# A second self attention whose negated maxima are written into the score banks by ScalarE

## What is computed

```
q = (q_in @ wq).reshape(b, n, H, HD).transpose(0, 2, 1, 3)
...
scores = jnp.einsum('bhnd,bhld->bhnl', q, k) * scale
probs = jax.nn.softmax(scores, axis=-1)
out = jnp.einsum('bhnl,bhld->bhnd', probs, v)
out = out.transpose(0, 2, 1, 3).reshape(b, n, H * HD)
return out @ wo + bo
```

## Time and profile before

| | us |
|---|---|
| median of 3 runs | 4218.95 |
| lowest and highest | 4212.62, 4226.44 |
| span of the profiled execution | 4217.9 |
| TensorE busy | 3909.5 (93%) |
| VectorE busy | 2770.9 (66%) |
| GpSimd busy | 1859.2 (44%) |
| ScalarE busy | 1839.2 (44%) |

### The profile page before, as it was taken

How to read it: one execution, slowest core, us unless ns; L and a number is a source line. 1 busy time by engine, 2 the same in 40 slices (tenths; PEclk the granted TensorE clock), 3 DMA queues, 4 the chain that set the end, 5 groups by cost and what they waited for, 6 DMA issues and landing times. The chain is left out here.

```text
span 4217.9 us, 64445 instructions
## 1 busy us (share of the span) xinstructions
PE 3909.5 (93%) x24639; PEld 2598.3 (62%) x24639; DVE 2770.9 (66%) x4547; ACT 1839.2 (44%) x2746; POOL 1859.2 (44%) x1203
## 2 busy tenths in 40 slices
PE   3799999994998997998999999999999979999899
PEld 2533443433557886884666666666666647777787
DVE  6599999953536654435676767676766737665665
ACT  1267777771443333442333333333333334444333
POOL 1288970001203002005777777877787753222200
PEclk9789999996779998997999999999999989999899
DMA  4734434405622005883211111121112010000100
GB/s 159 180 56 77 59 57 48 42 2 94 102 43 52 22 13 197 306 308 103 75 51 51 64 63 51 51 76 51 51 51 76 26 31 10 10 10 1 42 15 17
DMA packets 314421, 294.96 MB, mean 70 GB/s; under 512 B 133420, under 2 KB 237292, under 8 KB 313860
## 3 DMA queue, kind: packets, MB, share of 16 engines
q1 hardware_dynamic: 311460, 281.88, 25.7%
q0 software_dynamic: 2656, 8.97, 0.7%
HBM read 161.92 MB, written 127.28 MB: 69 GB/s over the span
## 5 line engine op out<-in xcount | busy, mean ns | idle before, releaser
L1741 POOL TENSOR_TENSOR f_sums<-f_sums,f_probs 128x1024 f32<-128x1024 f32 x384 | 915.5, 2384 | 154.8 <-ACT f_probs L1860 117.1
L1860 ACT ACTIVATE f_probs<-f_st 128x1024 f32<-128x1024 f32 x512 | 525.0, 1027 | 938.7 <-PE f_st L1906 933.9
L1758 DVE TENSOR_REDUCE f_mx<-f_s 128x1 f32<-128x512 f32 x1024 | 659.8, 686 | 380.7 <-PE f_s L1883 369.4
L1369 DVE TENSOR_REDUCE f_mx<-f_s 128x1 f32<-128x512 f32 x1024 | 638.6, 683 | 50.8 <-PE f_s L1501 28.4
L1481 ACT ACTIVATE f_probs<-f_st 128x512 f32<-128x512 f32 x1024 | 535.9, 601 | 225.6 <-PE f_st L1518 225.5
L1883 PE MATMUL f_s<-f_k,f_q 64*128 64x512 f32 x3072 | 515.0, 415 | 18.6 <-DMA f_k<-k 12.5
L1906 PE MATMUL f_st<-f_q,f_k 64*128 64x512 f32 x3072 | 485.2, 390 | 1.1 <-ACT f_probs L1860 1.0
L1920 PE MATMUL f_acc<-f_probs,f_v 128*64 128x512 f32 x2048 | 465.0, 596 | 0.0
L1883 PEld LDWEIGHTS f_s<-f_k,f_q 64*128 64x128 f32 x3072 | 341.2, 189 | 166.6 <-issue 112.1
L1906 PEld LDWEIGHTS f_st<-f_q,f_k 64*128 64x128 f32 x3072 | 366.4, 184 | 25.9 <-ACT f_probs L1860 3.8
L1518 PE MATMUL f_st<-f_q,f_k 50*128 50x512 f32 x1024 | 332.7, 472 | 6.9 <-ACT f_probs L1481 6.8
(11 more groups left out here) (320 smaller groups left out, 7874.5 us busy)
## 6 DMA issues: line engine op xcount, KB each, us to landing
q<-f_stage SPq DMA_DIRECT2D x80, 512.0 KB, 2.9
k<-f_stage SPq DMA_DIRECT2D x80, 512.0 KB, 2.9
f_q<-q SPq DMA_DIRECT2D x32, 1024.0 KB, 5.0
f_k<-k SPq DMA_DIRECT2D x32, 1024.0 KB, 7.3
v<-f_v_stage SPq DMA_DIRECT2D x64, 256.0 KB, 3.1
f_v<-v SPq DMA_DIRECT2D x32, 512.0 KB, 8.5
f_q<-q SPq DMA_DIRECT2D x96, 128.0 KB, 4.2
f_k<-k SPq DMA_DIRECT2D x96, 128.0 KB, 6.9
```

The lines of the kernel that those rows point to most:

```text
L1369: v.tensor_reduce(mx[:, i % 2, c:c + 1], bank[u % 4][:, :], AX_X, ALU.max).then_inc(s_free, 1)
L1741: g_.tensor_tensor(out, out, probs[:, n % NP, :, :], ALU.add).then_inc(sum_done, 1)
L1758: v.tensor_reduce(mx[:, i % 2, c:c + 1], bank[u % 3][:, :], AX_X, ALU.max).then_inc(s_free, 1)
L1860: a_.activation(probs[:, s % NP, :, :], stb[s % 2][:, :, :], ACT.Exp, scale=L.scale).then_inc(p_ready, 1)
```

## The change

The fourth pass of `shifted` goes. In its place ScalarE copies the negated maxima, present on all 128 partitions in a new tile `shift`, into the double bank (`seed`) before the three passes, which now accumulate on it (`start=False`). The seed of slot n+2 is issued right after the exponential of slot n and waits for it; `shifted` waits for its seed. Four matmuls at the start (`prime`) write the banks once by TensorE. `turned` becomes one copy; `maxima` stores its 16x128 values in DRAM, waits, and loads them back on all partitions (1 MB). EARLY goes from 3 to 7, the turn from slot 15 to slot 10 (TURN), and SP's load of q and k is parted from that of v and waits for `st_ready` in place of `pv_done`. The offset of 2 in `p_ready` goes.

```diff
-        NP, DEPTH, GROUP, EARLY, RING0 = 8, 3, 4, 3, 3
+        NP, DEPTH, GROUP, EARLY, RING0, TURN = 8, 3, 4, 7, 3, 10
...
-            m = [sb(f"m{k}", [P, N], F32R) for k in two]
-            mones = sb("mones", [P, P], F32R)
+            shift = [sb(f"shift{k}", [P, 2, N]) for k in two]
...
                 def maxima(i):
                     par = i % 2
-                    sp.wait_ge(m_split, i + 1)
-                    for h in range(2):
-                        for r in range(2):
-                            row = 64 * h + r
-                            sp.dma_start(m[par][row:row + 1, :].bitcast(F32).rearrange("o (q t) -> o q t", t=P),
-                                         mm[par][h * QB:(h + 1) * QB, r, :]).then_inc(m_in[par], 16)
+                    sp.wait_ge(s_free, at["turn", i] + 1)
+                    if i >= 2:
+                        sp.wait_ge(m_in[par], 16 * (i // 2))
+                    sp.dma_start(self.shift[par].rearrange("(c t) -> c t", t=P), mm[par][:, :]).then_inc(m_out[par], 16)
+                    sp.wait_ge(m_out[par], 16 * (i // 2 + 1))
+                    if i >= 2:
+                        sp.wait_ge(seeded, (i - 1) * SLOTS)
+                    sp.dma_start(shift[par][:, :, :].rearrange("p h t -> p (h t)"), self.shift[par].partition_broadcast(P))\
+                        .then_inc(m_in[par], 16)
...
                 for i in range(STEPS):
                     if i + 2 < STEPS:
                         if i > 0:
+                            sp.wait_ge(st_ready, i * SLOTS)
+                        load(i + 2)
+                        if i > 0:
                             sp.wait_ge(pv_done, i * GROUP)
-                        load(i + 2)
+                        load_values(i + 2)
                     if i + 1 < STEPS:
                         maxima(i + 1)
...
-                    v.tensor_scalar(mm[par][:, 0, :].bitcast(U32), rows.bitcast(U32), HI12, None,
-                                    ALU.bitwise_and).then_inc(m_cut, 1)
-                    dve.wait_ge(m_cut, i + 1)
-                    v.tensor_tensor(mm[par][:, 1, :], rows, mm[par][:, 0, :], ALU.subtract).then_inc(m_split, 1)
-                    dve.wait_ge(m_split, i + 1)
-                    dve.sem_inc(s_free, 1)
+                    v.tensor_copy(mm[par][:, :], rows).then_inc(s_free, 1)
...
+                def seed(n):
+                    i, s = n // SLOTS, n % SLOTS
+                    half = s // KC
+                    if n >= 2:
+                        act.wait_ge(p_ready, n - 1)
+                    if s == 0:
+                        act.wait_ge(m_in[i % 2], 16 * (i // 2 + 1))
+                    a_.activation(stb[s % 2][:, :, :], shift[i % 2][:, :, half * HALF:(half + 1) * HALF], ACT.Copy).then_inc(seeded, 1)
...
+                act.wait_ge(primed, 1)
+                seed(0)
+                seed(1)
...
                         a_.activation(probs[:, s % NP, :, :], stb[s % 2][:, :, :], ACT.Exp, scale=L.scale).then_inc(p_ready, 1)
+                        if n + 2 < STEPS * SLOTS:
+                            seed(n + 2)
...
+                def prime():
+                    pe.wait_ge(q_in[0], 32)
+                    for k in two:
+                        for h in range(2):
+                            ins = t.matmul(stb[k][:, h, :], k_[0][:, 0, 0:P], q[0][:, 0, 0:HALF], start=True, stop=True)
+                    ins.then_inc(primed, 1)
+
                 def shifted(i, s):
-                    cur, par, half, c = i % DEPTH, i % 2, s // KC, s % KC
-                    if s == 0:
-                        pe.wait_ge(m_in[par], (i // 2 + 1) * 64)
-                    pe.wait_ge(p_ready, i * SLOTS + s + 1)
+                    cur, half, c = i % DEPTH, s // KC, s % KC
+                    pe.wait_ge(seeded, i * SLOTS + s + 1)
                     cols, keys = slice(half * HALF, (half + 1) * HALF), slice(c * P, (c + 1) * P)
-                    for r, (kk, qq) in enumerate(((0, 0), (0, 1), (1, 0), (None, None))):
+                    for r, (kk, qq) in enumerate(((0, 0), (0, 1), (1, 0))):
                         for h in range(2):
                             rows = slice(64 * h, 64 * h + 64)
-                            lhs = mones[rows, :] if kk is None else k_[cur][rows, kk, keys]
-                            rhs = m[par][rows, cols] if kk is None else q[cur][rows, qq, cols]
-                            ins = t.matmul(stb[s % 2][:, h, :], lhs, rhs, start=r == 0, stop=r == 3, tile_position=(64 * h, 0))
+                            ins = t.matmul(stb[s % 2][:, h, :], k_[cur][rows, kk, keys], q[cur][rows, qq, cols], start=False, stop=r == 2,
+                                           tile_position=(64 * h, 0), skip_group_check=True)
...
+                prime()
                 for j in range(2 * QB):
                     pair(0, j)
...
+                        if s == TURN and i + 1 < STEPS:
+                            turn(i + 1)
                         if s == 15:
-                            if i + 1 < STEPS:
-                                turn(i + 1)
                             if i > 0:
                                 project(2 * i - 1)
```

More of the change, by code:

```diff
@@ L115, in __init__ @@
         self.rden = dram("rden", (B * H, N))
+        self.shift = dram("shift", (2, 2 * N))
         self.wq = {}
@@ L1623, in attend_wide @@
                     unit("den", i, 0)
-                if s == 15 and i + 1 < STEPS:
+                if s == TURN and i + 1 < STEPS:
                     unit("turn", i + 1)
@@ L1645, in attend_wide @@
             negm = sb("negm", [P, 2 * QB])
-            mm = [sb(f"mm{k}", [2 * QB, 2, P]) for k in two]
+            mm = [sb(f"mm{k}", [2 * QB, P]) for k in two]
             on = sb("on", [P, 2, HALF])
@@ L1657, in attend_wide @@
             q_in, v_in = [sem(f"q_in{k}") for k in slots_of], [sem(f"v_in{k}") for k in slots_of]
-            m_in = [sem(f"m_in{k}") for k in two]
+            m_out, m_in = [sem(f"m_out{k}") for k in two], [sem(f"m_in{k}") for k in two]
             w_in, b_in, w_high, w_low = sem("w_in"), sem("b_in"), sem("w_high"), sem("w_low")
             s_ready, s_free = sem("s_ready"), sem("s_free")
-            negm_done, m_cut, m_split = sem("negm"), sem("m_cut"), sem("m_split")
+            negm_done, primed, seeded = sem("negm"), sem("primed"), sem("seeded")
             st_ready, p_ready, pv_done = sem("st_ready"), sem("p_ready"), sem("pv_done")
@@ L1669, in load @@
                 def load(i):
-                    slot, b, g = i % DEPTH, i // L.ng, i % L.ng
+                    slot = i % DEPTH
                     row = slice(i * P, (i + 1) * P)
@@ L1673, in load, with load_values @@
                     sp.dma_start(k_[slot][:, :, :].bitcast(F32), self.k[:, row, :].rearrange("s p t -> p s t")).then_inc(q_in[slot], 16)
+                def load_values(i):
+                    slot = i % DEPTH
                     rows = self.v.rearrange("(r d) -> r d", d=P)[i * N:(i + 1) * N, :]
@@ L1678, in maxima @@
                     par = i % 2
-                    sp.wait_ge(m_split, i + 1)
-                    for h in range(2):
-                        for r in range(2):
-                            row = 64 * h + r
-                            sp.dma_start(m[par][row:row + 1, :].bitcast(F32).rearrange("o (q t) -> o q t", t=P),
-                                         mm[par][h * QB:(h + 1) * QB, r, :]).then_inc(m_in[par], 16)
+                    sp.wait_ge(s_free, at["turn", i] + 1)
[7 more added lines that the diff above has]
+                        .then_inc(m_in[par], 16)
                 load(0)
+                load_values(0)
                 sp.dma_start(wraw[:, :, :], wo.rearrange("(g p) d -> p g d", p=P)).then_inc(w_in, 16)
                 load(1)
+                load_values(1)
                 sp.dma_start(bias[:, :], bo.partition_broadcast(P)).then_inc(b_in, 16)
-                sp.wait_ge(set_done, 6)
                 maxima(0)
@@ L1702, in _ @@
                 g_ = nc.gpsimd
-                for k in two:
-                    g_.memset(m[k][:, :].bitcast(F32), 0.0).then_inc(set_done, 1)
-                g_.memset(mones[:, :].bitcast(F32), 0.0).then_inc(set_done, 1)
-                pool.wait_ge(set_done, 3)
-                for h in range(2):
-                    g_.memset(mones[64 * h:64 * h + 2, :].bitcast(F32), 1.0).then_inc(set_done, 1)
-                    pool.wait_ge(set_done, 4 + h)
                 g_.memset(ones[:, :], 1.0).then_inc(set_done, 1)
@@ L1734, in _ @@
                             n = half * KC + c
-                            pool.wait_ge(p_ready, i * SLOTS + n + 1 + 2)
+                            pool.wait_ge(p_ready, i * SLOTS + n + 1)
                             if c == 1:
@@ L1769, in turned @@
                     if i >= 2:
[L1770 to L1776 removed]
+                        dve.wait_ge(m_out[par], 16 * (i // 2))
+                    v.tensor_copy(mm[par][:, :], rows).then_inc(s_free, 1)
                 def invert(n):
```

(13 more changed lines are left out.)

2 lines of the change are left out of this document (removed).

## The result

The changed kernel takes 4233.15 us (median; 4220.73 to 4240.27) where the kernel before takes 4219.73 (4204.98 to 4234.44) beside it. The ratio is 1.0025, with a 95% interval of 1.0013 to 1.0036: 10.5 us slower, between 5.5 and 15 (the two medians are 13.4 apart). I had forecast 4245, 26 us slower. The direction is right, the size under half.

The account below looks back on a forecast made before the run. TensorE was taken to bound the kernel; steady groups +10.8, head +9.7, step 0 +1.9 and tail +4.0 sum to +26.4 us on a 4217.9 us span: 4245 on the median, own range 4225 to 4270, whole range 4212 to 4294.

Parts of the forecast that it names:

- The mechanism: In each four-slot group, ScalarE's chain of exponentials and seeds delays slot d to 5.10 us after slot a, against 4.88.
- the steady term: 120 ordinary groups at +0.09 us each: +11 us, with ends -25 and +49.
- the head: Start of the stage: priming 1.7 us plus four more early pairs at 2.01 us, sum +9.7 us.
- the tail: Groups without pairs in steps 30 and 31, +1.7 us a group before hiding: sum +4.0 us.
- VectorE's banks: Reductions delay a pair's second head 0.1 to 0.2 us; quick slots end near 4.8 us, under 5.10: costed at nothing.
- The turn in slot 10: Its bank joins the quick slots; the pair ends near 5.0 us, just covered; if not, 31 x 0.3 = 9 us.
- Step 0: Seven slots without a burst go at ScalarE's pace, 2.02 us against 1.63: about +1.9 us beyond two ordinary groups.
- rival 5: TensorE's clock falls because it now pauses; 5% of the stage at half clock gives 4320 us; chance 0.03.
- rival 1: ScalarE's PSUM write or its wait on its own result costs 0.2 us more: +75 us, 4294; chance 0.14.
- rival 2: Seeds are cheap, 0.95 us with no gap; not slower: -9 us, 4210; chance 0.12.
- rival 3: The removed passes come through whole as the seeds hide: -118 + 12 us, 4113; chance 0.04.
- rival 4: The maxima's broadcast is late, over 14 us; at 17 us some +90 + 26, 4335; chance 0.05.

Follow-up runs that it names:

- half reductions: The changed kernel with VectorE's reductions reading 256 of a bank's 512 columns: 4225.0 us with seeds, 4096.0 us with the seeds also removed (one run each).
- half seeds: The changed kernel with seeds of 512 elements in place of 1024, the first pass overwriting the bank: 4193.25 us, ratio 0.9943.
- the late turn: The changed kernel with EARLY 4, the turn in slot 13 and the priming matmuls after step 0's 16 pairs: 4230.3 us, ratio 1.0026.
- the hybrid: The changed kernel with seeds only for slots a and b, the fourth pass back in c and d, turn in slot 11: 4216.35 us, ratio 0.9991.
- the turn in the burst: The changed kernel with the turn in slot 11, ahead of the burst's sums and values, in place of slot 10: 4236.0 us, ratio 1.0037.

## Why the prediction was right or wrong, point by point

**The mechanism held.** The forecast said that the chain exponential, seed, exponential, seed takes the place of TensorE in each group. The 0.05 us between the last seed and slot d, the groups' 11.18 with half reductions and the fall to 10.81 with half seeds show it. It holds for three groups of four; in the group with the turn another path ends last, as below. ScalarE is busy 32.94 us in a step, near the 34 forecast.

**The step that failed is the steady term, which was mis-sized: +0.09 us a group forecast, -0.05 measured in the group that the forecast took.** Of the 13 us between forecast and stage, 10 are in steps 1 to 29. Two terms of the sum were off. The chain is 5.04, not 5.10: exponential plus gap is 1.06 and 1.04 us, not 1.08, as the gap is 0.03 rather than 0.05, and a seed is 1.03 rather than 1.05 (0.02 goes back, as the second exponential starts 0.07 before the seed's end, not 0.11). And where the stalled slot d is followed by sums, 2602.46 - 2601.55 = 0.91 us pass between their starts, against 2601.70 - 2600.58 = 1.12 before: 0.21 back, not the 0.13 that I took from a place where another pass of the same shape follows. 5.04 - 4.88 - 0.21 = -0.05. Over 116 groups that 0.14 us is 16 us. A difference of two lengths of five microseconds was priced from single links to within 0.05 us each, and four such links add up to more than the answer; my own ends (-0.21 to +0.41) said so. That the sign of the whole came out right is owed to the head and the tail: the steady steps, forecast at +10.4 us, gave +0.4.

The Trainium skill (ScalarE: Activation LUTs, the section "Step-by-step: what each stage is for") says that ScalarE is faster into PSUM than into SBUF. This case agrees in sign: 1029 ns for the seed, 1048 for the Copy of the same shape in SBUF, whose output type is another. It is 0.02 us, too little for the rival.

**VectorE's banks, costed at nothing, were worth nothing only behind the chain.** I put three quick slots at 4.8 us, under 5.10. Without seeds a group of 10.81 is 0.42 shorter than before's 11.23, where half reductions give 0.97: the banks hold 0.55 us a group as soon as the chain is gone. The "to the fore" of the text was right.

**The turn in slot 10, costed at nothing, costs 0.23 us a step.** This step failed too: the pairs with VectorE's banks and the turn, not the seed, end last there. TensorE in the turn's group, timeline:
```profile
2619.64 0.86 PE L1920 MATMUL f_st<-f_q,f_k 64*128 64x512 f32 x6
...
2622.68 1.07 PE L1920 MATMUL f_st<-f_q,f_k 64*128 64x512 f32 x6
2623.68 0.28 PE L1904 MATMUL f_s<-ident,f_negm 128*16 128x128 f32 x1
2623.89 1.30 PE L1894 MATMUL f_s<-f_k,f_q 64*128 64x512 f32 x6
2624.80 1.09 PE L1920 MATMUL f_st<-f_q,f_k 64*128 64x512 f32 x6
```
Slot d is at 5.16 us, 0.17 after its seed was there (ScalarE's ended at 2624.63). The turn starts 1.00 us after slot c and the sums 1.01 after slot d; with half reductions both take 0.90, the turn is still there, and the chain covers it. Without seeds slot d stands at 5.16 in this group as well, with neither seeds nor full reductions at 4.65. So the 0.23 us are the turn and the banks together, and no seed's. The text's "if not, 31 x 0.3 = 9 us" was the measured 31 x 0.23 = 7. It ate what the other groups won: 29 x (-0.05 - 0.04 + 0.18 - 0.07) = +0.6 us by the rounded groups, +0.4 measured.

**The head: +9.7 forecast, +5.3 measured, and the step was right at the clock it took.** The priming took 1908.58 - 1906.60 = 1.98 us (forecast 1.7). At the same clock the head is 51.1 - 41.1 = +10.0. The clock rose on the way in after's profiled run, which I had not allowed for, as the profile of before showed a low one up to the end. How often it rises there in the timed runs the profiles don't tell, so how much of the 10.5 us is head stays unknown.

**Step 0:** +1.2 against +2.1, the same two smaller terms.

**The tail: +4.2 forecast with its two usual groups, +6.5 measured.** The first group of step 31 takes 12.05 us, not 10.54, while with the late turn it takes 10.48. TensorE there:
```profile
3390.22 1.65 PE L1920 MATMUL f_st<-f_q,f_k 64*128 64x512 f32 x6 [1.03 <-ACT f_st L1844]
3391.80 1.97 PE L1944 MATMUL f_s<-f_sums,f_ones 128*64 128x512 f32 x4
3393.56 3.64 PE L1935 MATMUL f_acc<-f_probs,f_v 128*64 128x512 f32 x16
```
and its window:
```profile
3376.00:3390.00 14.00, 9.70 (x58) 5.05 (x58) 1.38 (x2) 11.20 (x12) 11.37 (x6) 1.00 0.01 1
3390.00:3394.00 4.00, 3.77 (x12) 1.54 (x14) 0.18 (x1) 3.94 (x5) 3.86 (x2) 0.57 0.00 0
```
After 14 us in which TensorE was busy for 9.70, the granted clock stood at 0.57 for 4 us; slot d and the sums took 1.58 + 1.76 us where 2 x 0.91 are usual: 1.5 us. The third group of the step (12.11) lost as much, with a granted clock of 0.52 from 3414 to 3417 us. Without the two the tail would have been some 3 us shorter, under the forecast.

That is rival 5, small and in the tail alone; I had read 1.00 in before's tail, where TensorE pauses less (35.19 of 36.00 us busy).

**The rivals.** Dear links (rival 1) fell with 0.03 and 0.05 us. Cheap seeds (rival 2) fell as it was worded, at 1.03 us, but the 0.21 on the other side took a group to -0.05 us, part of the way to its breakeven of -0.13. The passes did not come through whole (rival 3), for the reason given, and even without seeds they don't, for a second that I hadn't weighed: VectorE holds half of it back. The broadcast (rival 4) was in time. SyncE's queue:
```profile
2624.38 0.32 SPq L1685 DMA_DIRECT2D shift<-f_mm  x1
2625.74 0.33 SPq L1689 DMA_DIRECT2D f_shift<-shift  x1
```
It lands some 4.7 us after 2625.74, and the first seed that needs it starts only after 2637.56, 7 us later. With the turn three slots later the margin is gone for ScalarE, and for TensorE 1 to 2 us of it are left in most steps.

**Open:** what sets the clock level in the head of a run; whether the priming matmuls have a part in it; how the head varies over the timed runs.

## What to carry to other kernels

Before costing a removed pass at its count, list all that follows the engine at the same pace: here VectorE's banks stood 0.37 us a group behind ScalarE's chain, and TensorE 0.55 behind them; only with both gone did the 0.97 us come through. A wait in the profile is no cost by itself: ScalarE's wait for the broadcast appeared with the late turn together with a longer group, and had next to nothing to do with it. Look whether the engine that bounds the stage waited too. An accumulator's initial value written by another engine puts two more links in the bank's cycle (read, then write again); with the two banks here it won time only where a burst hid it (the hybrid's slots a and b), and in all too little to be told from nothing. When a forecast is a small difference of two long chains, give the sum of the links' uncertainties as its size, and take the time of a step from a row with the same neighbours on both sides.

## What the runs showed of the hardware

- Four matmuls that wrote the two double banks once, at the start, were enough for all 512 slots: the scores are added to what ScalarE has written there, in after and in the seeded runs that compute the whole.
- Links between engines: a seed of 128x1024 in 1029 ns; 0.03 us from an exponential's end to the seed that waits for it on the same engine, 0.05 from a seed's end to the scores that wait for it.
- A change of tile shape on TensorE costs: one more burst of 128x64 matmuls between 64x128 ones about 0.48 us in before, in three parts (0.22 on entering, 0.21 with the burst, 0.10 behind it).
- The head of the stage ran at either clock level from run to run with nearly the same work in it: 16 pairs at 2.01 us each in before and with the late turn, at 1.52 without seeds and with the turn in the burst, a mix in after and in before with EARLY 7. In the runs that went at 1.52 all through, the pairs after the turn's pause of 3.56 us between reductions came at 2.01 again; with the late turn, whose first 16 went at 2.01, they came at 1.52.
